# Graph layers on one core: ScalarE's group lag taken out of the first node stage, tables cleared and gather indices staged ahead

## The reference, cut to what matters

```python
x = _layernorm(x + rgcn(x, edges, 16 relations))        # two relational convolutions
x = _layernorm(x + gat(x, edges, 8 heads))              # h = x @ lin_w.T, attention per edge
x = _layernorm(x + relational(x, src, dst, 8 relations))
x = _layernorm(x + sage(x, edges))
```

## Time and profile before

| what | value |
|---|---|
| median of 3 runs | 5724.4 us (5715.57 to 5733.77) |
| profiled execution, its own time | 5718.69 us |
| its span, first to last instruction | 5716.9 us, mean granted TensorE clock 0.845 |
| busy share of the span | PE 74%, DVE 48%, ACT 32%, POOL 69% |

### The profile page before, as it was taken

How to read it: one execution, slowest core, us unless ns; L and a number is a source line. 1 busy time by engine, 2 the same in 40 slices (tenths; PEclk the granted TensorE clock), 3 DMA queues, 4 the chain that set the end, 5 groups by cost and what they waited for, 6 DMA issues and landing times. The chain is left out here.

```text
span 5716.9 us, 112497 instructions
## 1 busy us (share of the span) xinstructions
PE 4215.4 (74%) x25852; PEld 3469.8 (61%) x25853; DVE 2727.5 (48%) x10258; ACT 1841.3 (32%) x5188; POOL 3963.6 (69%) x4080
## 2 busy tenths in 40 slices
PE   5688888887887888746666666766666666998887
PEld 3577777776777777635555555555555554665655
DVE  8743433334444443256666665644544446334323
ACT  0122222223333333334444444544444443001001
POOL 3077777766777777377777776477777775775765
PEclk6699999999999999856565666888888888999998
DMA  3166666652222222133333333223323234555544
GB/s 87 48 172 154 163 151 162 154 146 71 65 66 66 56 62 66 56 82 84 84 83 84 81 85 75 67 90 94 95 88 101 88 100 140 179 189 187 177 164 143
DMA packets 379514, 615.32 MB, mean 108 GB/s; under 512 B 117582, under 2 KB 287087, under 8 KB 366447
## 3 DMA queue, kind: packets, MB, share of 16 engines
q1 hardware_dynamic: 247631, 342.12, 20.1%
q0 software_dynamic: 126976, 263.71, 18.0%
q10 hardware_dynamic: 4128, 1.75, 0.1%
HBM read 527.37 MB, written 79.86 MB: 106 GB/s over the span
## 5 line engine op out<-in xcount | busy, mean ns | idle before, releaser
L1544 PE MATMUL PS<-ROOM 128*128 128x128 f32 x8320 | 1044.6, 282 | 130.3 <-ACT ROOM L1116 99.5
L1544 PEld LDWEIGHTS PS<-ROOM 128*128 128x128 f32 x8320 | 985.6, 196 | 189.9 <-ACT ROOM L1116 107.6
L933 POOL DMA_INDIRECT GB<-table,IDX x832 | 804.5, 967 | 300.0 <-issue 252.3
L1116 ACT COPY ROOM<-PS 128x512 f32<-128x512 f32 x1040 | 610.1, 587 | 920.4 <-PE PS L1560 919.4
L933 POOL DMA_INDIRECT GB<-in_x,IDX x416 | 405.4, 974 | 294.9 <-ACT IDX L1086 158.8
L1560 PE MATMUL PS<-OH,GB 128*128 128x256 f32 (+1 forms) x1664 | 378.0, 391 | 235.7 <-DMA GB<-table,IDX 173.5
L893 POOL DMA_INDIRECT H<-table_gat,IDX x416 | 427.7, 1028 | 126.8 <-issue 125.0
L893 POOL DMA_INDIRECT GB<-table_gat,IDX x416 | 412.5, 992 | 127.6 <-issue 122.5
L933 POOL DMA_INDIRECT ROOM<-table,IDX x416 | 411.4, 989 | 126.8 <-issue 125.9
L933 POOL DMA_INDIRECT H<-in_x,IDX x416 | 403.1, 969 | 126.8 <-issue 126.5
L1560 PEld LDWEIGHTS PS<-OH,GB 128*128 128x128 f32 x1664 | 315.9, 236 | 288.4 <-issue 219.1
(11 more groups left out here) (438 smaller groups left out, 7819.1 us busy)
## 6 DMA issues: line engine op xcount, KB each, us to landing
neighbours<-ROOM SPq DMA_DIRECT2D x32, 1700.0 KB
ROOM<-neighbours SPq DMA_DIRECT2D x32, 1700.0 KB
PACK<-neighbours SPq DMA_DIRECT2D x32, 1700.0 KB
H<-one_over SPq DMA_DIRECT2D x416, 128.0 KB
ROOM<-one_over SPq DMA_DIRECT2D x416, 128.0 KB
ROOM<-local_row SPq DMA_DIRECT2D x104, 256.0 KB
GB<-table,IDX POOLq DMA_INDIRECT x1152
ROOM<-table,IDX POOLq DMA_INDIRECT x736
```

The costliest lines, as they stand in the source:

```text
L933: pool.indirect_dma_start(out=r.rows[c][:, j * P:(j + 1) * P], out_offset=None, in_=r.dram[:, :], in_offset=bass.IndirectOffsetOnAxis(ap=I ...
L1116: act.copy(to.rearrange("p r (j d) -> p r j d", j=r.per), of.rearrange("p (j d r) -> p r j d", j=r.per, d=NEAR))\
L1544: ins = nc.tensor.matmul(PS[:, 4, 0:P], r.near[1 - b][:, t * P:(t + 1) * P], r.weights[:, t * P:(t + 1) * P], start=t == 0, stop=t == r.re ...
```

## The change

- Node stage: ScalarE takes squares, root and scaling of the same group, with no group behind; it scales blocks 0 and 1 of a group, and VectorE scales blocks 2 and 3, right after its inversion. SyncE's store of a group now waits for both engines.
- GpSimd clears `aux` before the node stage (after the last strip of near_b), and `sums` group by group as TensorE has read it. The waits on the clears count 14 instead of 2.
- ScalarE stages the first indices of near_b before `h_rows`, those of near_c before the copies of line 1308, and those of the attention loop before its waits.
- The wait of near_b's gathers for `root_ps` moves to the third batch of each round of four.

```diff
@@ SyncE
             for g in range(GROUPS):
                 sp.wait_ge(n0_lin, g + 1)
+                sp.wait_ge(n0_x, g + 1)
                 sp.dma_start(table_gat[columns_of(g), :]..., lin_rows(g)).then_inc(t_gat.stored[0], 16)
@@ GpSimd
-            def gather_near(r):
+            def gather_near(r, third=None):
                         pool.wait_ge(near_idx, k + (r.first + 1))
                         pool.sem_inc(near_passed, 1)
+                        if third and c == 2:
+                            pool.wait_ge(*third)
+                            pool.sem_inc(near_passed, 1)
...
             pool.wait_ge(h_stored, 16 * GROUPS)
-            pool.wait_ge(root_ps, GROUPS)
-            gather_near(near_b)
-            pool.wait_ge(n0_ps, GROUPS)
+            gather_near(near_b, (root_ps, GROUPS))
             pool.wait_ge(made_out, 16 * BESIDE_B)
+            pool.wait_ge(mx_hot, B_TILES + 1)
             pool.memset(aux[0:2 * HEADS, :], 0.0).then_inc(gat_zeroed, 1)
-            pool.memset(sums, 0.0).then_inc(gat_zeroed, 1)
+            for g in range(GROUPS):
+                pool.wait_ge(n0_ps, g + 1)
+                pool.memset(sums[:, 4 * g * P:(4 * g + 4) * P if g < GROUPS - 1 else NODES_P], 0.0).then_inc(gat_zeroed, 1)
             gather_gat(r_gat)
@@ ScalarE
             run_near(step)
+            stage, step = near_round(near_b)
+            for c in range(FOUR):
+                stage(c, c)
             for g in range(GROUPS):
                 act.wait_ge(h_ps, g + 1)
...
-            stage, step = near_round(near_b)
-            for c in range(FOUR):
-                stage(c, c)
             act.wait_ge(h_stored, 16 * GROUPS)
...
-            for g in range(GROUPS + 1):
+            for g in range(GROUPS):
 ...
-                    act.wait_ge(n0_inv, g)
-                    for n, q in enumerate(blocks_of(g - 1)):
-                        ins = act.activation(lin_rows(g - 1)[:, n, :], n0_products(g - 1, n), ACT.Copy, ...)
+                act.wait_ge(n0_inv, g + 1)
+                for n, q in enumerate(blocks_of(g)[0:2]):
+                    ins = act.activation(lin_rows(g)[:, n, :], n0_products(g, n), ACT.Copy, scale=inv_root[:, q:q + 1])
+                ins.then_inc(n0_lin, 1)
...
             act.activation(RE[:, :], one[0:HEADS, :], ACT.Exp)
-            act.wait_ge(gat_zeroed, 2)
-            act.wait_ge(t_gat.stored[0], 16 * t_gat.stores)
             for c in range(3):
                 stage_gat(c, c)
+            act.wait_ge(gat_zeroed, 1 + GROUPS)
+            act.wait_ge(t_gat.stored[0], 16 * t_gat.stores)
...
+            stage, step = near_round(near_c, True)
+            for c in range(FOUR):
+                stage(c, c)
@@ VectorE
                 dve.wait_ge(n0_inv, g + 1)
+                for n, q in enumerate(blocks[2:], 2):
+                    dve.tensor_scalar(lin_rows(g)[:, n, :], n0_products(g, n), inv_root[:, q:q + 1], None, ALU.mult)
```

More of the change, by code:

```diff
@@ L789, in _ @@
             sp.wait_ge(logits_out, 16)
-            sp.wait_ge(gat_zeroed, 2)
+            sp.wait_ge(gat_zeroed, 1 + GROUPS)
             sp.wait_ge(pen_zero, 1)
@@ L1198, in _ @@
             act.wait_ge(added, 2 * BATCHES)
-            for g in range(GROUPS + 1):
[L1200 to L1208, removed]
-                    act.wait_ge(n0_inv, g)
-                    for n, q in enumerate(blocks_of(g - 1)):
-                        ins = act.activation(lin_rows(g - 1)[:, n, :], n0_products(g - 1, n), ACT.Copy,
-                                             scale=inv_root[:, q:q + 1])
-                    ins.then_inc(n0_lin, 1)
+            for g in range(GROUPS):
+                act.wait_ge(n0_ps, g + 1)
+                for n, q in enumerate(blocks_of(g)):
+                    ins = act.activation(unread(q), n0_centered(g, n)[:, NL:], ACT.Square, accum_out=squares[:, q:q + 1])
+                ins.then_inc(n0_root, 1)
+                act.wait_ge(n0_root, 2 * g + 1)
+                here = slice(blocks_of(g)[0], blocks_of(g)[-1] + 1)
+                act.activation(root[:, here], squares[:, here], ACT.Sqrt, bias=eps[:, 0:1], scale=1.0 / P).then_inc(n0_root, 1)
+                act.wait_ge(n0_inv, g + 1)
+                for n, q in enumerate(blocks_of(g)[0:2]):
+                    ins = act.activation(lin_rows(g)[:, n, :], n0_products(g, n), ACT.Copy, scale=inv_root[:, q:q + 1])
+                ins.then_inc(n0_lin, 1)
             def acc_copy(k, b):
@@ L1319, in residual @@
                         .then_inc(res_act, 1)
-            stage, step = near_round(near_c, True)
-            for c in range(FOUR):
-                stage(c, c)
             act.wait_ge(keyed, KEYED)
@@ L2377, in _ @@
             dve.wait_ge(pen_zero, 1)
-            dve.wait_ge(gat_zeroed, 2)
+            dve.wait_ge(gat_zeroed, 1 + GROUPS)
             def ahead(k, b, at_i):
```

## The result

The changed kernel takes **5641.99 us** (median of 4, 5639.08 to 5643.86) against 5724.8 (median of 4, 5715.57 to 5733.77): ratio 0.9855, 95% interval 0.984 to 0.9869. The profiled execution takes 5641.5 us, 77.2 less than that of before; its span is 5639.7.

What follows compares the result with a forecast made beforehand. GpSimd's gathers were taken to pace the three edge loops, with TensorE and ScalarE taking turns in the node stage between. Gains 9.0 + 40.5 + 12.5 = 62 us gave 5656.7 or 5662.4, stated as 5660; range 5642 to 5681.

Steps and rivals of the forecast that it cites:

- Near_b's start: Start of the near_b loop: indices staged earlier, first gather at 1300.8 instead of 1310.01; gain 9.0 us, between 8.5 and 9.8.
- The node stage's working: Node stage between near_b and attention: without the lag, period per group 2.9 us at full clock or 3.86 at half.
- 0.74 x 43.9 + 0.26 x 31.0 = 40.5: Node stage gain in us: 43.9 at clock 1.00 and 31.0 at 0.50, weighted by near_c's mean clock of 0.87.
- Near_c's start: Start of the near_c loop: gather 15.5 us earlier, less 3 for gathers beside VectorE's key work; gain 12.5, between 8.8 and 15.5.
- The 6 us: Start of near_c: most that gathers could lose if VectorE's clear and as much of casts all locked them out.
- What would show it: Closing list of trace signs, right or wrong: TensorE start spacing, gathers released by stores, cast at 0.58, batch times.
- 10.0, 10.5 and 10.4 us a batch unchanged: Sign of being right: the three edge loops near_b, attention and near_c keep their time per batch of eight gathers.
- The range's low end: Fastest time allowed, 5642: gains of 69 from the profiled execution give 5650, gathers 0.01 us cheaper in one loop 8 more.
- the attention loop's gathers stretch: Rival, chance 0.05: gathers in the attention loop get dearer as phase between engines changes; slower above 1.084 us a gather.
- twice the stretch: Attention loop case: gathers at 1.07 us, twice the present excess over near_b's 0.950, losing 49 of the 62 us.
- the clock didn't stay low: Rival, chance 0.11: TensorE's clock stays at 0.50 through the node stage, gain there only 31, time 5669.
- near_b and near_c are paced by their gathers: Denied by a rival, chance 0.10: other engines set these loops' rate, earlier gathers gain nothing, only 40.5 remains, 5681.

Runs made afterwards that it cites:

- near_b_old: Changed kernel with near_b's index staging back behind the scalings of the constants and the root_ps wait ahead of the loop again; 5652.65 us, ratio 0.9889.
- starts_only: Changed kernel with the node stage's loop of before, leaving the earlier staging for near_b and near_c and the clears by group; 5686.58 us, ratio 0.995.
- a_act: Changed kernel with all four scalings of a group on ScalarE and none on VectorE; 5642.73 us, ratio 0.9871.
- p24: Kernel before with only 24 idle VectorE instructions (semaphore increments) added ahead of the node stage; 5714.47 us, ratio 0.9995.
- near_c_old: Changed kernel with the staging of near_c's indices back behind the residual work, where it was before; 5656.18 us, ratio 0.9897.

## Why the prediction was wrong, point by point

**Near_b's start** (9.0): right. 8.9 in the trace; 9.1 by near_b_old's trace and 10.7 by its median.

**The node stage's working** (period 2.9 or 3.86): right, at full clock to the tenth. Squares to TensorE's start 2377.89 - 2374.24 = 3.65 us against 3.57; two new scalings 0.63 against 0.54; two groups 5.83 against 5.78; first to last start 2395.39 - 2360.33 = 35.1 against 34.8; last start to first gather 6.0 against 5.8. What was mis-sized is the step "0.74 x 43.9 + 0.26 x 31.0 = 40.5": the granted clock stayed at 1.00, with TensorE busy 26.21 of 37.30 us behind a near_b at 0.98, and the gain was 43.2. Taking the clock's mean from near_c, a loop of a thousand us, for a stage of 37 was the error. What the sum took VectorE's share to bring, nothing showed: without it the stage is as long, and 1.4 us shorter from TensorE's first start.

**Near_c's start** (12.5): mis-sized by the 3 us taken off for gathers beside VectorE's keys. The first gather comes 13.8 us earlier behind the attention loop in the changed kernel, 15.3 and 15.5 in starts_only and a_act. The first gathers take 0.99 and 1.10 us where an undisturbed one takes 0.94; the first twelve lose 0.4 us together, and those that begin inside VectorE's clear of 2.89 us lose nothing:

```profile
3618.10 2.89 DVE L2674 MEMSET ROOM<- 128x3400 uint32 x1 [0.65 <-issue]
3618.48 0.94 POOL L937 DMA_INDIRECT GB<-table,IDX  x1 [0.30 <-issue]
3619.73 0.95 POOL L937 DMA_INDIRECT GB<-table,IDX  x1 [0.30 <-issue]
```

The 6 us that the Trainium skill's rule (SBUF — State Buffer, "Who interferes with whom") was taken to cost were not there either. Its other half held: VectorE's two scalings from PSUM take 0.62 us beside a clear (at 2364.29) and 0.63 without one (at 2372.36).

**The step that failed** stands under "What would show it" and is silent in the sum: "10.0, 10.5 and 10.4 us a batch unchanged", and no term at all for the loops behind near_c. The attention loop lost 15.7, mix_b with its end gained 23.9; together +8.2, on top of 69.0 from the parts against 62. What they depend on, the place of VectorE's code behind 24 added instructions, the prediction put at nothing without a reason. The range's low end had 8 us for cheaper gathers "in one loop" and so took in nearly all of the sum by luck: neither of the two sizes was in it.

**The rival "the attention loop's gathers stretch"** came true in part: 855.87 / 832 = 1.029 us a gather against 1.009. Its cause was another. It was put down to the phase between the loop's two beginnings, but a_act and p24 show that VectorE's 24 instructions do it, as far as the traces show through the phase of a single product in each round. Its price, 15.7 us, is a third of the 49 that twice the stretch would have cost. The other rivals fell: the clock didn't stay low, and near_b and near_c are paced by their gathers, near_b_old and near_c_old show it.

The rule behind the stretch is the same section of the Trainium skill: a VectorE instruction with two inputs in SBUF and a GpSimd instruction that reads SBUF shut each other out, and the first to issue keeps the ports. The rows agree for the gather: the one at 2877.31, ahead of its product by 0.18 us, takes 0.94, the one at 2834.17, 0.39 behind, 1.65. For the product they don't: the one at 2877.49, begun under a gather, takes 1.21 like any other. The prediction used the section for near_c's casts and not for the one instruction of 1.22 us that runs in every batch.

Of the medians: before was 5724.8 in 4 runs but 5714.75 to 5716.97 in 14, 17 and 7 later ones, so some 9 us of the 82.8 may be the first sample's (the changed kernel was not timed again); 5716 - 5642 = 74 agrees with the 77.2 of the traces within the spread of before.

## What to carry to other kernels

An edit that adds or drops instructions on an engine shifts all its later code; in loops where that engine shows idle time put down to "issue" in the middle of a body, take the sum of those stops as a bound for that shift, plus or minus (here 29 us of stops at the addition for 20 us of mix_b, 92 us for 16 to 18 of the attention loop), and tell it from the edit itself by as many idle instructions in the old kernel. Compare stages the edit doesn't touch before trusting a total: here two of them moved by -15.7 and +23.9 us and nearly hid each other. Where GpSimd's gathers pace a loop, look for VectorE instructions of two SBUF inputs of a microsecond or more beside them, and try them in a few pieces: here four were worth 46 us of loop.

## What was not expected of the hardware

- 24 idle instructions on VectorE change a later edge loop by 19 us, 256 by little (421.9, 402.5, 425.3); the packets of code in the attention loop go with it (125, 149, 125), and VectorE's long stops end 1.5 to 1.95 us behind such a packet.
- A gather begun under a VectorE product of 128x1024 takes up to 1.75 us and ends 0.82 behind the product, one begun 0.18 us ahead of it takes 0.94, and the product takes 1.20 to 1.26 in all eleven traces that have it in one piece; under four pieces of 128x256 the mean is 1.08, under eight of 128x128 it is 1.10 again.
- The granted clock held 1.00 through a node stage in which TensorE was busy 70%, where the same stage at 55 to 61% had fallen to 0.50 after 12 us.
